# Last two items of a 32-item attention pipeline issued by a hand-written ending, last layer norm done batch by batch

## The chip, the core and the metric

One Trainium2 chip, one of its cores. The engines are PE (TensorE: matmuls and transposes, its weight loads shown as PEld), DVE (VectorE), ACT (ScalarE), POOL (GpSimd) and SP (SyncE, which here only issues DMAs). The metric is the device time of one launch in microseconds (us). A change is called faster or slower when the median moves by over 1%; less than that a measurement of this kernel can hardly tell from none.

## The reference, cut to what is computed

Eight batches of 128 tokens, model width 128, 16 heads. Four attention layers follow each other on `x`; the fourth, `L3`, is where the change lies. Its queries come from `x`, keys and values from `ctx_1024`, and its result goes through a layer norm that is the kernel's output.

```python
qh = jnp.einsum('bsd,hde->bhse', q, Wq) + bq[None, :, None, :]
kh = jnp.einsum('bsd,hde->bhse', k, Wk) + bk[None, :, None, :]
vh = jnp.einsum('bsd,hde->bhse', v, Wv) + bv[None, :, None, :]
scores = jnp.einsum('bhse,bhte->bhst', qh, kh) / scale          # E = 8 numbers a head
attn = jax.nn.softmax(scores, axis=-1)
ctx = jnp.einsum('bhst,bhte->bhse', attn, vh)
out = cat @ Wo + bo
x = q + out
mu = jnp.mean(x, axis=-1, keepdims=True)
var = jnp.mean((x - mu) ** 2, axis=-1, keepdims=True)
return (x - mu) * jax.lax.rsqrt(var + LN_EPS) * gamma + beta
```

## The kernel before

One attention of one batch is an item: `n = 0..31`, layer `n // 8`, batch `b = n % 8`. Items 24 to 31 are L3, and item 31 (`LAST` in the change) is the last. A further layer with 64-number heads runs between items 7 and 8 and is not touched. All engines walk the same list of steps `s`, each with its own in-order instruction stream, and meet by semaphores only; nothing is scheduled at run time. From step 25 on item `n` enters at step `s = n + 1` (step 24 is a hole), and the stages of an item are spread over the steps by the functions `pe_attn`, `act_attn`, `pool_attn` and `dve_attn`:

- step n+1: PE forms the scores in two halves of eight heads, S(n,0) into PSUM banks 0 and 1 and S(n,1) into banks 2 and 3; DVE takes the row maxima of each half (`dve_max`, counted by `max_done`); POOL splits the maxima into three bf16 parts (`pool_split`).
- step n+2: PE turns the split maxima (`pe_mT`, L345), ACT copies them (`act_mrow`), PE forms the transposed scores T(n,0) in banks 4 and 5 (`pe_scores`, L322 the products, L330 the maxima subtracted), ACT takes the exponential (`act_exp`, L415).
- step n+3: T(n,1) goes to the same banks 4 and 5 and so waits until the exponential of T(n,0) has read them; then V(n), the product with the values, 32 matmuls (`pe_V`, L364), into bank 6 for even and 7 for odd items (`o_bank`).
- step n+4: ACT copies the sum out (`act_osum`, L422), PE turns it back (`pe_back`, L372), DVE divides by the row sums (`dve_norm`, L496 and L500), PE turns it once more (`pe_onT`, L377), ACT copies (`act_onT`, L428).
- step n+5: PE multiplies by the output weights (`pe_z`, L381), DVE adds the residual and takes mean and variance (`dve_z` and `dve_stats`, L508, L514, L516).

`free` holds PE back until the maxima of the half that last used a bank are taken, before other work borrows that bank. The queries of L3 are made in pairs of batches at steps 24, 26, 28 and 30 (`pe_proj`, L592, into bank 2): ACT rounds them to bf16 (`act_p0`), DVE forms the rest (`dve_rest`, L666), ACT and DVE the next two parts (L674, L680), and SP and ACT issue the DMAs that stack the parts in `qs` (`stack_dma`, L692). Step 30 makes those of batches 6 and 7, that is of items 30 and 31, so S(30,0) waits for these DMAs.

The final layer norm goes by pairs of batches: at even steps 30 to 36 POOL computes (variance + eps)^-0.5 for two batches (`pool_rstd`, L550 and L552), and at the end of odd steps 31 to 37 DVE's `output(b0)` does two normalisations (L569) and a multiplication and an addition over both batches (L1636, L1638). SP then stores the two batches, 64 KB each (L1055), behind all its other DMAs.

The steps end as they run empty: at step 34 PE has T(31,1), back(30), z(29), onT(30), V(31); at step 35 back(31), z(30), onT(31); at step 36 z(31).

## Time and profile before

| what | value |
|---|---|
| time, median of 3 runs | 343.07 us (342.51 to 345.08) |
| the profiled execution, its own time | 343.29 us |
| its span, first to last instruction | 341.4 us |
| PE / DVE / ACT / POOL busy | 86% / 69% / 62% / 27% |
| granted TensorE clock, mean | 0.982 |

The profile is of one execution. Its span is 1.9 us shorter than that execution's own time, and that time is 0.2 us above the median. Busy shares are averages over layers with different limits; for the change only the last 40 us matter.

### The profile page before, as it was taken

The numbers are of one execution on the slowest core, as the hardware profiler recorded it, in microseconds if no ns is written. First come the engines' busy times: TensorE is split into PE (matmuls) and PEld (weight loads), VectorE is DVE, ScalarE is ACT, GpSimd is POOL, SyncE is SP. The second block draws the span as 40 slices with busy tenths as digits, with TensorE's granted clock in tenths as the row PEclk, the third lists the DMA queues.
The fourth block names the chain that finished last, engine by engine and source line by source line (L and its number), as shares of the span: only waits on it lengthen the run. The fifth ranks groups of instructions, "written<-read, shape, count | busy, mean of one in ns | idle before, by whom it ended". The sixth has DMA issues, their size and how long they took to land.

```text
span 341.4 us, 10348 instructions
## 1 busy us (share of the span) xinstructions
PE 293.8 (86%) x4157; PEld 220.2 (64%) x4157; DVE 236.7 (69%) x480; ACT 212.9 (62%) x463; POOL 92.7 (27%) x261
## 2 busy tenths in 40 slices
PE   7889999988989989988988899889869986996871
PEld 4535657766868768866766676666547764784650
DVE  6566498259886666767766578787886657775855
ACT  4377778666677776876755666457655544555550
POOL 3025353110310000001413734514433304314131
PEclk9999999999999999999999999999998999999896
DMA  6879900000000000001320324312330011011001
GB/s 198 233 182 243 356 6 2 2 2 0 2 2 2 2 0 2 2 0 42 84 64 25 85 80 134 104 49 78 110 93 3 8 44 48 4 46 49 17 18 31
DMA packets 26735, 20.93 MB, mean 61 GB/s; under 512 B 3256, under 2 KB 25664, under 8 KB 26432
## 3 DMA queue, kind: packets, MB, share of 16 engines
q1 hardware_dynamic: 23360, 18.24, 19.0%
q10 hardware_dynamic: 3328, 2.04, 2.1%
q8 instruction: 33, 0.54, 0.7%
q14 instruction: 14, 0.11, 0.1%
HBM read 6.11 MB, written 0.52 MB: 19 GB/s over the span
## 4 chain that ended last, share of the span: by engine, by line
PE 48%; ACT 15%; DVE 12%; issue 7%; POOL 5%; SPq 5%; DMA 4%; ACTq 2%; POOLq 0%
PE psum L364 7%; ACT probs L867 5%; PE psum L825 4%; SPq L692 4%; DMA qs<-part_q 4%; PE psum L791 4%; PE psum L766 4%; PE psum L740 3%; ACT probs L875 3%; PE psum L322 3%; PE psum L337 3%; PE psum L592 3%; PE psum L986 2%; PE psum L802 2%; PE psum L817 2%
## 5 line engine op out<-in xcount | busy, mean ns | idle before, releaser
L489 DVE TENSOR_REDUCE maxs<-psum 128x8 f32<-128x1024 f32 x64 | 77.5, 1213 | 37.4 <-PE psum L337 28.6
L415 ACT ACTIVATE probs<-psum 128x1024 f32<-128x1024 f32 x64 | 65.6, 1025 | 34.6 <-PE psum L330 21.8
L364 PE MATMUL psum<-probs,vpad 128*32 128x128 f32 x1024 | 35.4, 280 | 0.0
L867 ACT ACTIVATE probs<-psum,maxs 128x128 f32<-128x128 f32 x128 | 34.8, 390 | 0.5 <-DVE maxs L916 0.5
L364 PEld LDWEIGHTS psum<-probs,vpad 128*32 128x32 f32 x1024 | 26.6, 111 | 12.0 <-issue 6.9
L337 PE MATMUL psum<-ks,qs 64*128 64x128 bf16 x512 | 25.7, 221 | 9.9 <-DMA qs<-part_q 3.3
L322 PE MATMUL psum<-qs,ks 64*128 64x128 bf16 x512 | 25.7, 221 | 8.4 <-ACT probs L415 8.2
L550 POOL TENSOR_SCALAR rstd<-stats 128x2 f32<-128x2 f32 (+1 forms) x19 | 4.2, 223 | 99.8 <-DVE stats L516 99.7
L322 PEld LDWEIGHTS psum<-qs,ks 64*128 64x128 bf16 x512 | 14.6, 95 | 21.8 <-ACT probs L415 10.8
L926 DVE TENSOR_REDUCE mres<-probs 128x8 f32<-128x1024 f32 x16 | 19.5, 1218 | 12.6 <-ACT probs L867 12.6
L916 DVE TENSOR_REDUCE maxs<-psum 128x8 f32<-128x1024 f32 x16 | 19.5, 1220 | 11.7 <-PE psum L791 11.7
L467 POOL CAST mp<-maxs 128x16 bf16<-128x16 f32 x32 | 6.6, 206 | 74.9 <-DVE maxs L489 74.5
L337 PEld LDWEIGHTS psum<-ks,qs 64*128 64x128 bf16 x512 | 16.8, 96 | 14.8 <-issue 8.1
L330 PE MATMUL psum<-mrow,sel 64*128 64x128 bf16 x512 | 25.2, 219 | 0.0
L875 ACT COPY probs<-psum 128x1024 f32<-128x1024 f32 x16 | 16.7, 1046 | 5.8 <-PE psum L802 5.8
L930 DVE TENSOR_TENSOR probs<-probs,mres 128x1024 f32<-128x1024 f32 x16 | 19.6, 1225 | 0.6
L422 ACT COPY osum<-psum 128x256 f32<-128x256 f32 x32 | 12.1, 377 | 12.5 <-PE psum L364 12.3
L817 PE MATMUL psum<-probs,v1all 128*64 128x128 f32 x256 | 17.5, 279 | 2.3 <-ACT probs L875 1.8
L552 POOL TENSOR_TENSOR rstd<-rstd,small 128x2 f32<-128x2 f32 (+1 forms) x23 | 18.0, 780 | 1.9
L330 PEld LDWEIGHTS psum<-mrow,sel 64*128 64x128 bf16 x512 | 17.8, 95 | 0.5
L766 PE MATMUL psum<-xnT,wmat 128*128 128x256 f32 x64 | 17.4, 400 | 0.3 <-ACT ks L773 0.3
L817 PEld LDWEIGHTS psum<-probs,v1all 128*64 128x64 f32 x256 | 13.7, 136 | 5.9 <-ACT probs L875 4.6
(159 smaller groups left out, 627.8 us busy)
## 6 DMA issues: line engine op xcount, KB each, us to landing
qs<-part_q SPq DMA_DIRECT2D x63, 64.0 KB, 2.0
ks<-part_k SPq DMA_DIRECT2D x30, 128.0 KB, 2.4
ks<-part_k SPq DMA_DIRECT2D x36, 64.0 KB, 2.0
wmat<-in_wmat SPq DMA_DIRECT2D x1, 1856.0 KB, 10.5
qs<-part_q ACTq DMA_DIRECT2D x21, 64.0 KB, 2.2
wmat<-in_wmat SPq DMA_DIRECT2D x1, 1024.0 KB, 7.0
qs<-part_q SPq DMA_DIRECT2D x6, 128.0 KB, 5.2
wrow<-in_wrow SPq DMA_DIRECT2D x1, 704.0 KB, 8.6
```

What stands on the lines that cost most here:

```text
L322: e.matmul(bank(4 + r)[:, bt(c)], ks[M.slot][rows, i, bt(b)], qs[rows, i, bt(b)], start=(c == 0), stop=False, skip_group_check=True)
L330: mm = e.matmul(bank(4 + a)[:, bt(i)], sel[rows, mhalf, i, :], mrow[rows, m % 2, :], start=False, stop=True, skip_group_check=True)
L337: s_mm = e.matmul(bank(2 * half + r)[:, bt(c)], qs[rows, i, bt(b)], ks[L.slot][rows, i, bt(b)], start=(c == 0), stop=L is not L2, skip_gro ...
L364: mm = e.matmul(o_bank(n)[rg(c), bt(half)], vpad[:, n % 2, 4 * half + c, G * a:G * a + G], pt, start=(a == 0), stop=(a == 1), skip_group_c ...
L415: e.activation(probs_of(n, half), bank(4, 2), ACT.Exp, scale=layer(n).scale)\
L489: e.tensor_reduce(maxs[:, n % 2, 8 * half:8 * half + 8], bank(2 * half, 2).rearrange("p (h k) -> p h k", k=P), AX.X, ALU.max, negate=True)\
L766: mm = e.matmul(bank(chunk_bank(i, name, c))[:, t * PAIR:(t + 1) * PAIR], a1[:, 2 * (2 * c + t) + KIND[name], :], src[:, i * PAIR:(i + 1) ...
L817: mm = e.matmul(bank(6)[HD * pp:HD * pp + HD, bt(t)], v1[:, b, h * HD:(h + 1) * HD], pT[:, half, bt(4 * pp + t)], start=True, stop=True)
L867: ins = e.activation(probs[:, half, bt(s)], bank(2 * half, 2)[:, bt(s)], ACT.Exp, bias=maxs[:, b % 2, 8 * half + s:8 * half + s + 1])
L875: e.copy(pT[:, half, :], bank(4, 2)).then_inc(L1("pT_out"), 1)
L916: e.tensor_reduce(maxs[:, b % 2, 8 * half:8 * half + 8], bank(2 * half, 2).rearrange("p (h k) -> p h k", k=P), AX.X, ALU.max, negate=True)\
L930: e.tensor_tensor(p8, p8, rec.unsqueeze(2).broadcast_to([P, 8, P]), ALU.mult).then_inc(L1("norm"), 1)
```

## The change

`LAST = 31`. PE, ACT and DVE leave the common step functions after step 33; three hand-written endings (`pe_end`, `act_end`, the last lines of DVE's stream) issue what is left. T(31,1) is written right behind T(31,0) into banks 0 and 1 in place of 4 and 5, and waits only until the maxima of S(31,0) are taken. V(31) is written into bank 2 in place of 7, its wait for item 29's sum to be read is gone, and its second half alone waits for the second exponential. The two last items then go in pairs: back(30), back(31), onT(30), onT(31), z(30), z(31).

The final norm is regrouped for all of L3's batches. DVE computes (x - mean) * gamma as soon as a batch's statistics are there (`scaled`), POOL computes one batch's factor a step (steps 29 to 36), and DVE's `output(b)` multiplies by it and adds beta; SP stores each batch when it is ready. In steps 29 to 33 `scaled(s - 29)` stands ahead of the query work of `end_of_even` and ahead of the maxima of the second half, and `output(s - 29)` behind them.

```diff
         def probs_of(n, half):
             return probs[:, 2 * (n % 2) + half, :]
 
+        LAST = N_ITEM - 1
+
         def o_bank(n):
-            return bank(6 + n % 2)
+            return bank(2 if n == LAST else 6 + n % 2)
 
         def m_turned(n):
             return bank(3)[:, 0:P // 2].bitcast(BF16)
...
             for what, count in FREED.get((n, half), []):
                 e.wait_ge(what, count)
 
+        def t_bank(n, half):
+
+            return 0 if (n, half) == (LAST, 1) else 4
+
         def T_ready(e, n, half):
+            if (n, half) == (LAST, 1):
+                e.wait_ge(sem("max_done"), 2 * LAST + 1)
+                return
             if n == 0 and half == 0:
                 e.wait_ge(sem("maskbc"), 3)
                 e.wait_ge(*L0.mm_done("q_rest", 2))
...
         def pe_scores(e, n, half, m, mhalf):
 
             if m is not None:
-                M, b = layer(m), m % B
+                M, b, tb = layer(m), m % B, t_bank(m, mhalf)
                 T_ready(e, m, mhalf)
                 for c, r, rows, i in heads(mhalf):
-                    e.matmul(bank(4 + r)[:, bt(c)], ks[M.slot][rows, i, bt(b)], qs[rows, i, bt(b)],
+                    e.matmul(bank(tb + r)[:, bt(c)], ks[M.slot][rows, i, bt(b)], qs[rows, i, bt(b)],
                              start=(c == 0), stop=False, skip_group_check=True)
                 if M is L2:
                     pe_mask(e, 4, 1, False)
...
                 for i in range(4):
                     for a in range(2):
                         rows = slice(HD * a, HD * a + HD)
-                        mm = e.matmul(bank(4 + a)[:, bt(i)], sel[rows, mhalf, i, :], mrow[rows, m % 2, :],
+                        mm = e.matmul(bank(tb + a)[:, bt(i)], sel[rows, mhalf, i, :], mrow[rows, m % 2, :],
                                       start=False, stop=True, skip_group_check=True)
                 mm.then_inc(sem("T_mm"), 1)
             if n is not None:
...
             e.transpose(m_turned(n), mp[:, n % 2, :], identB[:, :]).then_inc(sem("mT_mm"), 1)
 
         def pe_V(e, n):
-            e.wait_ge(sem("exp_done"), 2 * n + 2)
+            if n != LAST:
+                e.wait_ge(sem("exp_done"), 2 * n + 2)
             e.wait_ge(sem("vpad_in"), n + 1)
-            if n >= 2:
+            if n >= 2 and n != LAST:
                 e.wait_ge(sem("z_read"), n - 1)
             if n == 0:
                 e.wait_ge(sem("k_raw"), 3)
...
             if n == B + 1:
                 e.wait_ge(*L2.mm_done("q_rest", 4))
             for half in range(2):
+                if n == LAST:
+                    e.wait_ge(sem("exp_done"), 2 * n + 1 + half)
                 for a in range(2):
                     for c in range(4):
                         pt = probs_of(n, half)[:, bt(2 * c + a)]
...
             for s in steps:
                 n, n1, n2 = at(s, lo, hi), at(s - 1, lo, hi), at(s - 2, lo, hi)
                 n3, n4 = at(s - 3, lo, hi), at(s - 4, lo, hi)
+                if n2 == LAST:
+                    break
                 pe_scores(e, n, 0, n2, 1)
                 ahead(s)
                 if n1 is not None:
...
                 if n4 is not None:
                     pe_z(e, n4)
                 pe_scores(e, n, 1, n1, 0)
+                if n1 == LAST:
+                    pe_scores(e, None, 1, LAST, 1)
                 if n3 is not None:
                     pe_onT(e, n3)
                 odd(s)
...
                     pe_V(e, n2)
 
 
+        def pe_end(e):
+
+            pe_z(e, LAST - 2)
+            pe_V(e, LAST)
+            pe_back(e, LAST - 1)
+            pe_back(e, LAST)
+            pe_onT(e, LAST - 1)
+            pe_onT(e, LAST)
+            pe_z(e, LAST - 1)
+            pe_z(e, LAST)
+
+        def act_end(e):
+
+            act_exp(e, LAST, 1)
+            act_osum(e, LAST - 1)
+            act_osum(e, LAST)
+            act_onT(e, LAST - 1)
+            act_onT(e, LAST)
+
         def act_mrow(e, n):
             e.wait_ge(sem("mT_mm"), n + 1)
             if n >= 2:
...
             e.wait_ge(sem("T_mm"), 2 * n + half + 1)
             if n >= 2:
                 e.wait_ge(sem("V_mm"), n - 1)
-            e.activation(probs_of(n, half), bank(4, 2), ACT.Exp, scale=layer(n).scale)\
+            e.activation(probs_of(n, half), bank(t_bank(n, half), 2), ACT.Exp, scale=layer(n).scale)\
              .then_inc(sem("exp_done"), 1)
 
         def act_osum(e, n):
...
         def act_attn(e, steps, lo, hi, even, odd, first=lambda s, half: None):
             for s in steps:
                 n1, n2, n3 = at(s - 1, lo, hi), at(s - 2, lo, hi), at(s - 3, lo, hi)
+                if n2 == LAST:
+                    break
                 if n3 is not None:
                     act_osum(e, n3)
                 first(s, 0)
...
             for p in range(4):
                 stack_up(e, L3, "q", 2 * p, 2)
             for b in range(B):
-                e.wait_ge(sem("out_ready"), b // 2 + 1)
+                e.wait_ge(sem("out_ready"), b + 1)
                 e.dma_start(out_d[b], xn[:, b, :]).then_inc(sem("stored"), 16)
             e.wait_ge(sem("stored"), 16 * B)
 
...
                     pool_resid(e, "FF", "b_ff", b, 2, "stats_LC", b + 2)
                 if 24 <= s <= 30 and s % 2 == 0:
                     pool_resid(e, "L3", "bo_3", s - 24, 2, "ff_read", (s - 24) // 2 + 1)
-                if 30 <= s <= 36 and s % 2 == 0:
-                    pool_rstd(e, "N3", "L3", "ln", 1e-5, s - 30, 2)
+                if 29 <= s <= 36:
+                    pool_rstd(e, "N3", "L3", "ln", 1e-5, s - 29, 1)
 
             def behind2(s):
                 if s in (9, 11):
...
             pe_proj(e, L2, "k", 4, 2, 7)
             pe_proj(e, L2, "q", 4, 2, 7, PAIR)
             pe_attn(e, range(10, 37), B, N_ITEM, even2, odd2, ahead2)
+            pe_end(e)
 
         @block.scalar
         def _(e):
...
                     act_p1(e, L3, "q", s - 24, 2)
 
             act_attn(e, range(9, 37), B, N_ITEM, even2, odd2, first2)
+            act_end(e)
 
         @block.vector
         def _(e):
...
                 if 23 <= s <= 29 and s % 2:
                     dve_ff(e, (s - 23) // 2)
 
-            def output(b0):
-                bs, n = slice(b0, b0 + 2), b0 // 2
-                dve_xn(e, "N3", "ln", b0, 2)
-                e.wait_ge(sem("xn_N3"), b0 + 2)
-                e.tensor_tensor(xn[:, bs, :], xn[:, bs, :], row("g_3", 2), ALU.mult).then_inc(sem("aff3"), 1)
-                e.wait_ge(sem("aff3"), n + 1)
-                e.tensor_tensor(xn[:, bs, :], xn[:, bs, :], row("b_3", 2), ALU.add).then_inc(sem("out_ready"), 1)
+            def scaled(b):
+                e.wait_ge(sem("stats_L3"), b + 1)
+                e.scalar_tensor_tensor(out=xn[:, b, :], in0=x[:, b, :], scalar=stats[:, b, 0:1],
+                                       in1=row("g_3")[:, 0, :], op0=ALU.subtract, op1=ALU.mult)\
+                 .then_inc(sem("scaled3"), 1)
+
+            def output(b):
+                e.wait_ge(sem("rs_N3"), 2 * b + 2)
+                e.wait_ge(sem("scaled3"), b + 1)
+                e.scalar_tensor_tensor(out=xn[:, b, :], in0=xn[:, b, :], scalar=rstd[:, b:b + 1],
+                                       in1=row("b_3")[:, 0, :], op0=ALU.mult, op1=ALU.add)\
+                 .then_inc(sem("out_ready"), 1)
 
             def odd2(s):
                 if s == 9:
...
                 if 22 <= s <= 28 and s % 2 == 0:
                     for c in (2, 3):
                         dve_relu(e, (s - 22) // 2, c)
-                if 31 <= s <= 37 and s % 2:
-                    output(s - 31)
+                if 29 <= s <= 36:
+                    output(s - 29)
 
             def late(s):
                 if 21 <= s <= 27 and s % 2:
...
                     any_p2(e, LC, "q", s - 15, 2)
 
             def end_of_even(s):
+                if 29 <= s <= 36:
+                    scaled(s - 29)
                 if 24 <= s <= 30 and s % 2 == 0:
                     dve_rest(e, L3, "q", s - 24, 2, 2)
                     any_p2(e, L3, "q", s - 24, 2)
 
-            for s in range(9, 38):
+            for s in range(9, 34):
                 dve_attn(e, [s], B, N_ITEM, even2, odd2, first2, end_of_even)
                 late(s)
+            dve_z(e, LAST - 2)
+            scaled(B - 3)
+            dve_norm(e, LAST - 1)
+            dve_norm(e, LAST)
+            output(B - 3)
+            dve_z(e, LAST - 1)
+            scaled(B - 2)
+            dve_z(e, LAST)
+            scaled(B - 1)
+            output(B - 2)
+            output(B - 1)
 
 
 # ---- launch: one core; the host only lays the arrays out ----
```

## Rows read from the trace of the kernel before

**Rows 1.** The page's chain that ended last, over the whole span, by engine.

```profile
PE 48%; ACT 15%; DVE 12%; issue 7%; POOL 5%; SPq 5%; DMA 4%; ACTq 2%; POOLq 0%
```

**Rows 2.** Windows: busy us of each engine (instructions), granted clock, DMA share, GB/s.

```profile
315.00:320.00 5.00, 3.94 (x62) 3.20 (x66) 3.17 (x7) 2.47 (x4) 0.00 (x0) 0.66 0.01 3
...
316.00:317.00 1.00, 0.94 (x11) 0.75 (x12) 0.29 (x1) 0.13 (x2) 0.00 (x0) 0.50 0.00 0
...
335.00:342.00 7.00, 0.00 (x0) 0.00 (x0) 2.66 (x9) 0.00 (x0) 0.93 (x2) 0.59 0.13 37
```

**Rows 3.** Timeline of the last 15 us: start, duration, what [idle before <-releaser].

```profile
326.40 0.23 PE L345 MATMUL psum<-identB,mp 128*128 128x128 bf16 x1 [0.97 <-POOL mp L472]
...
327.68 1.02 ACT L415 ACTIVATE probs<-psum 128x1024 f32<-128x1024 f32 x1 [0.74 <-PE psum L330]
...
328.84 0.40 PE L322 MATMUL psum<-qs,ks 64*128 64x128 bf16 x8
...
330.80 1.08 PE L364 MATMUL psum<-probs,vpad 128*32 128x128 f32 x32
...
331.94 0.37 ACT L422 COPY osum<-psum 128x256 f32<-128x256 f32 x1 [0.79 <-PE psum L364]
...
334.16 0.49 PE L381 MATMUL psum<-wmat,onT 128*128 128x128 f32 x2 [0.36 <-ACT onT L428]
...
335.14 0.42 DVE L1638 TENSOR_TENSOR xn<-xn,wrow 128x256 f32<-128x256 f32 x1
335.48 0.28 DVE L508 TENSOR_TENSOR x<-psum,resid 128x128 f32<-128x128 f32 x1
...
336.13 0.18 DVE L516 BATCH_NORM_AGGREGATE stats<-stats 128x2 f32<-128x6 f32 x1
336.40 0.22 POOL L550 TENSOR_SCALAR rstd<-stats 128x2 f32<-128x2 f32 x1 [4.08 <-DVE stats L516]
...
337.45 0.60 DVE L569 TENSOR_SCALAR xn<-x,stats,rstd 128x128 f32<-128x128 f32 x2 [1.14 <-POOL rstd L552]
...
338.54 0.42 DVE L1638 TENSOR_TENSOR xn<-xn,wrow 128x256 f32<-128x256 f32 x1
```

**Rows 4.** The line L1055: issue ns min/median/max, first and last start.

```profile
L1055 SPq DMA_DIRECT2D out_x<-xn x8: 332/394/432, 321.9 to 339.4; - x8
```

**Rows 5.** The chain that ended last, 306 to 323 us: start, duration, what.

```profile
306.32 1.20 DVE maxs L489
...
308.83 0.58 PE psum L592 x4
...
311.06 0.47 DVE rest_q L666
...
312.57 3.44 DMA qs<-part_q
316.06 0.63 PE psum L337 x5
...
320.40 0.52 DVE xn L569 x2
...
321.75 0.74 DVE maxs L489
```

**Rows 6.** Timeline, near 46, 88 and 320 us.

```profile
46.61 0.65 DVE L1553 SCALAR_TENSOR_TENSOR xn<-x,stats,wrow 128x128 f32<-128x128 f32 x2
...
46.89 0.22 POOL L469 TENSOR_TENSOR mres<-maxs,mp 128x16 f32<-128x16 f32 x1
...
88.08 1.23 DVE L930 TENSOR_TENSOR probs<-probs,mres 128x1024 f32<-128x1024 f32 x1
88.14 1.74 POOL L552 TENSOR_TENSOR rstd<-rstd,small 128x2 f32<-128x2 f32 x1
...
320.84 0.39 PE L337 MATMUL psum<-ks,qs 64*128 64x128 bf16 x8
```

**Rows 7.** The page's DMA issues: count, KB each, median us to landing.

```profile
qs<-part_q ACTq DMA_DIRECT2D x21, 64.0 KB, 2.2
```

## The prediction, made before the kernel was run

> **What bounds the kernel now.** I read the profile in three steps. First the chain that ended last, by engine: the reader is to see that PE holds about half of it and no other engine a fifth [rows 1], so a PE average says little about the end. Second, windows over the last 40 us. While PE waits for stacked queries near 315 us its granted clock falls to 0.50, its lower level of 1.2 GHz; a mean of 0.66 over 315 to 320 us means some 3.4 us at that level [rows 2]; and in the last 7 us PE does nothing at all while DVE works 2.7 us and POOL 0.9 us [rows 2]. The end is therefore no matter of throughput but one chain of dependent small steps. Third, the timeline from 326 us, to see that chain. The maxima of item 31 reach PE at 326.40. T(31,1) starts at 328.84, right when the exponential of T(31,0) (327.68 to 328.70) has freed the banks; V(31) runs 330.80 to 331.88; z(31) is ready on PE at 334.65, but DVE takes it only at 335.48, because `output(4)` ends just before, at 335.56 with the overlap of the pipeline. Statistics end at 336.31, POOL's factor lets DVE go on at 337.45, `output(6)` ends at 338.96 [rows 3]. The last of the stores is issued at 339.4 [rows 4] and the span ends at 341.4.
>
> **Part 1, the ending on PE and ACT.** T(31,1) moves from 328.84 to right behind T(31,0), which ends near 327.6 (it is done before the exponential that starts at 327.68 [rows 3]). T is two groups of eight products, 0.40 us each as the profile models them [rows 3] and overlapping, so 0.4 to 0.8 us; I take 0.55, as groups of eight issue faster than they drain. It reaches banks 0 and 1, whose maxima were taken by 323 us [rows 5], so this wait is long met. Queued behind it on PE stand onT(29) and V(30), both 0.55 us later; V(30) then ends near 329.5. z(29) follows (0.25 us of PE's time, half of what z(31) shows with its drain [rows 3]), so V(31) starts near 329.75 in place of 330.80. Its first half needs only the exponential of 328.70; its second half comes at 330.3, and the second exponential, which ACT starts after a copy smaller than osum's 0.37, by 329.1, and which takes 1.02 us [rows 3], has ended by then. V(31) ends near 330.85: 1.05 us earlier. From V(31)'s end to z(31) ready took 334.65 - 331.88 = 2.8 us [rows 3]; that chain stays, and item 30's work is woven into its waits, so z(31) is ready near 333.6 (333.5 to 334.1 if each interleaved transpose delays the other).
>
> **Part 2, DVE's order at the end.** `output(4)` no longer stands ahead of z(31). z(30) is ready near 333.1: its turn back starts when V(31) ends at 330.85 and its chain from there is that of item 31 before, from 332.31 (osum's end) to 334.65, 2.3 us [rows 3]. DVE then does z(30) with statistics, 0.83 us (335.48 to 336.31 [rows 3]), and `scaled(6)`, priced by two instructions of the same form that take 0.65 us together, at 0.34 us with its hand-over [rows 6]. So z(31) starts near 334.25, where before it was 335.48: 1.2 us gained, and DVE, not PE, is what is late there. Its statistics end at 335.1. POOL's two instructions plus both hand-overs took 337.45 - 336.31 = 1.14 us [rows 3]; for one batch I take the same, since two numbers a row are already nearly nothing (0 to 0.3 us less is the bound). `scaled(7)`, 0.34 us, lies under POOL's 1.14 and costs nothing; without that cover it would cost its 0.34. `output(7)` starts at 336.25.
>
> Here a row and a rule differ. Where DVE runs the same scalar_tensor_tensor form, POOL's L469 inside it takes 0.22 us, as short as L550 with DVE idle [rows 3, 6]; where DVE runs a long tensor_tensor on two SBUF inputs, POOL's L552 takes 1.74 us, while at the end both of POOL's instructions with their hand-overs take 1.14 [rows 3, 6]. The Trainium skill, page "SBUF — State Buffer", the section on the memory's two separate sides, says that a DVE instruction with two SBUF inputs and a GpSimd instruction that reads SBUF exclude each other for a whole instruction, whoever starts first. By that rule `scaled(7)`, which is released by the same statistics as POOL, would hold POOL up by about 0.3 us on the last chain; by the row of the same form it costs nothing. I go by the row, and hold 0.3 us in the range.
>
> **Part 3, the last norm and its store.** From POOL's factor to the end of `output(6)` took 338.96 - 337.45 = 1.51 us [rows 3]; one `output(7)` takes 0.34 as above: 1.17 us gained. Before, two stores were issued one behind the other after that; batch 6 now goes 0.8 us earlier, and the median issue of 0.39 us is gained [rows 4]. From the last issue to the end of the span stays 341.4 - 339.4 = 2.0 us. Sum of the ending: 1.23 + 1.17 + 0.4 = 2.8 us; that is, the span would end at 338.6. With the bounds above (0.5 for the interleaving on PE, 0.3 for the port, 0.3 of POOL's own time the other way) it is 2.0 to 3.1.
>
> **Part 4, what steps 29 to 33 pay.** The norm's work for batches 0 to 3 was at steps 31 and 33, 1.44 us each: two L569 (0.60), L1636 and L1638 (0.42 each) [rows 3]. Now each step from 29 carries 0.34 + 0.34. Steps 29 and 30, which had none, lie on the chain. At step 29 `scaled(0)` stands ahead of the maxima that start at 306.32; POOL's split, the turn on PE and, behind it on PE's queue, the query product at 308.83 all follow from them [rows 5]. `scaled(0)` must also await the statistics, which the maxima need not (they start 0.1 us before those end), so the price is about 0.38. At step 30 `scaled(1)` stands right ahead of `dve_rest` at 311.06 [rows 5], and the ACT copy, the DMA issues and S(30,0) at 316.06 wait for that: another 0.38. `output(0)` and `output(1)` stand behind the maxima, in time in which DVE idles until PE's next scores, and cost nothing (0.34 each if that idle time is gone). POOL's new factors at steps 29 and 31 stand ahead of the splits, but take about 1.0 us while DVE's maxima take 1.2, so they are hidden; without that cover 1.0 us each.
>
> At step 31 the maxima of S(31,0) start at 321.75, held back by `output(0)` of 320.40 on [rows 5]; S(31,0) itself had ended on PE at 321.23 [rows 6], 0.5 us before. There 1.44 us goes and 0.34 comes, but `scaled(2)` delays the earlier maxima by 0.38 and with them POOL's split: the two nearly cancel, and `scaled(3)` at step 32 adds 0.38 behind a start that is 0.1 to 0.4 earlier. I take +0.15 for these two steps (0 to 0.5). At step 33 `scaled(4)` and `output(4)` fit before item 30 comes back near 331. Last, SP's stores: two now follow directly behind the query DMAs, whose last lands 3.44 us after its issue [rows 5]. No row shows a store beside them; from below it is 0, from above 64 KB, one issue of 0.4 us. I take 0.1.
>
> Sum of the price: 0.38 + 0.38 + 0.15 + 0.1 = 1.0 us (0.5 to 1.7).
>
> **Forecast.** -2.8 + 1.0 = -1.8 us. The profiled execution would go from 343.29 to 341.5; it stood 0.2 above the median, so 341.3 for the median, 0.5% less than before. That is under the 1% that a measurement of this kernel can tell.
>
> **Rivals.**
> (A) The early price is absorbed. The last query DMA took 3.44 us where those from ACT's queue have a median of 2.2 [rows 7]; if something other than DVE's rest sets its landing, the 0.76 us disappears and with the best ending the gain is 2.8 to 3.1: 340.1. For it: that landing is odd. Against: its issue follows ACT and DVE without a gap.
> (B) The ending gives less: the pairwise order on PE makes each item wait for the other's copy and the port rule holds. Then z(31) is 0.5 later and POOL 0.3 later, so 2.0 is gained against 1.0 paid: 342.1. For it: five hand-overs between PE, ACT and DVE in 2.8 us; against: V(31) is a full 1.05 us earlier whatever follows.
> (C) Slower than before. The place is PE's wait for the query DMAs at 314 to 316 us. It grows by 0.8 to 1.2 us, and this wait is what precedes the stretch at clock 0.50. The scores' group takes 0.63 us there, and 0.40 at full clock [rows 3, 5]. If the low level lasts one more stretch of the same 3.4 us, over PE's densest work of step 31 and 32, it costs up to half of it, 1.7 us, and with the price at its upper end of 1.7 the loss of 3.4 exceeds the gain of 2.8: 343.7 (343.07 + 0.6). With that price it decides once the low stretch is over 2.2 us longer. Against: one longer idle stretch has already cost its clock, and the wait's start doesn't move.
> (D) The change doesn't do what it says, T(31,1) or V(31) held by a wait that I overlook: part 1 is gone, part 3 keeps its 1.57 and part 2 perhaps 0.2: 343.07 - 1.8 + 1.0 = 342.3, which looks like B.
>
> **How the numbers follow.** Forecast 0.48, A 0.20, B with D 0.20, C 0.12. The forecast's own band is 340.7 to 341.9. The range takes in A with its lower end and run-to-run scatter of the medians of 0.5 us, and most of B and C: 339.5 to 343.4. Over 1% faster means below 339.64: only the far end of A together with scatter, 0.13. Over 1% slower means above 346.5, which no case reaches alone: 0.03. The rest, 0.84, is within 1%.
>
> **What the changed profile would show.** Right: V(31) starting near 1.05 us after V(30)'s end less z(29), with the second exponential done before its second half; PE's last matmul 1 us or more nearer to the turn of item 31's maxima; one DVE instruction, not four, after the last POOL factor; one store issued at the end; about 12.2 us from that turn to the end of the span, where it was 15.0. Step 29's maxima start 0.4 us later behind their scores, and S(30,0) about 0.8 us later in the span. Wrong: a wait of POOL beside `scaled(7)`, an idle DVE before z(31), or S(30,0) no later than 316.1. The forecast fails if steps 29 to 32 pay over 2 us, or if the clock's low stretch grows.

## The result and the profile after

The change brings the median from 342.9 us (12 runs, 339.25 to 345.08) to 340.83 us (12 runs, 339.59 to 342.52): ratio 0.9949, 95% interval 0.9927 to 0.9971. That is less than the 1% from which a change is called faster here; the interval does leave out 1, so the gain is small but there. The ratio leaves out slow executions and is not the quotient of the medians. A second, later measurement of both kernels gave 0.9927 (0.9886 to 0.9968). The profiled execution took 341.1 us with a span of 339.2; 341.3 was forecast for the median.

First the page's chain that ended last, by engine, and two windows over the stretches of [rows 2] (columns as there).

```profile
PE 45%; ACT 15%; DVE 12%; SPq 7%; issue 7%; DMA 6%; POOL 6%; ACTq 2%; POOLq 0%
```

```profile
315.00:320.00 5.00, 3.06 (x69) 2.37 (x72) 2.32 (x6) 3.37 (x7) 0.85 (x4) 1.00 0.16 44
...
335.00:340.00 5.00, 0.00 (x0) 0.00 (x0) 1.68 (x7) 0.00 (x0) 1.61 (x4) 0.62 0.09 26
```

The low clock of [rows 2] is missing in this execution: 1.00 where 0.66 was, though PE waits as long for its queries (5.00 us from the query rest to S(30,0) in both). From 335 us on PE is idle as before, DVE works 1.68 us there in place of 2.66, and POOL 1.61 in place of 0.93, since it now computes one factor for each batch. Now the timeline of the last stretch, the answer to [rows 3]; lines have moved: L354 is the turn of the maxima (L345 before), L331 T's products, L450 the exponential, L376 V, L457 osum, L393 z, L545 the sum, L553 the statistics, L587 and L589 POOL's factor, L1673 `scaled`, L1680 `output`.

```profile
327.18 0.23 PE L354 MATMUL psum<-identB,mp 128*128 128x128 bf16 x1 [1.21 <-POOL mp L509]
...
328.25 0.39 PE L331 MATMUL psum<-qs,ks 64*128 64x128 bf16 x8
...
328.45 1.03 ACT L450 ACTIVATE probs<-psum 128x1024 f32<-128x1024 f32 x1 [0.74 <-PE psum L339]
...
330.48 1.08 PE L376 MATMUL psum<-probs,vpad 128*32 128x128 f32 x32
...
331.62 0.37 ACT L457 COPY osum<-psum 128x256 f32<-128x256 f32 x1 [0.80 <-PE psum L376]
...
333.33 1.01 PE L393 MATMUL psum<-wmat,onT 128*128 128x128 f32 x4
...
334.69 0.35 DVE L1673 SCALAR_TENSOR_TENSOR xn<-x,stats,wrow 128x128 f32<-128x128 f32 x1
...
334.95 0.28 DVE L545 TENSOR_TENSOR x<-psum,resid 128x128 f32<-128x128 f32 x1
...
335.60 0.18 DVE L553 BATCH_NORM_AGGREGATE stats<-stats 128x2 f32<-128x6 f32 x1
335.82 0.35 DVE L1673 SCALAR_TENSOR_TENSOR xn<-x,stats,wrow 128x128 f32<-128x128 f32 x1
335.87 0.37 POOL L587 TENSOR_SCALAR rstd<-stats 128x1 f32<-128x1 f32 x1
...
336.32 0.56 POOL L589 TENSOR_TENSOR rstd<-rstd,small 128x1 f32<-128x1 f32 x1
336.92 0.35 DVE L1680 SCALAR_TENSOR_TENSOR xn<-xn,rstd,wrow 128x128 f32<-128x128 f32 x1 [0.48 <-POOL rstd L589]
```

T(31,1) begins 0.2 us before the exponential of T(31,0), no longer behind it. Counted from the turn of item 31's maxima, V(31) starts after 3.30 us (4.40 before [rows 3]), DVE takes z(31) after 7.77 (9.08), and the span ends after 12.02 (15.0). One instruction follows POOL's last factor. The line of the stores, answer to [rows 4]:

```profile
L1092 SPq DMA_DIRECT2D out_x<-xn x8: 332/332/1777, 314.1 to 337.3; - x8
```

One store is left at the end: 339.2 - 337.3 = 1.9 us. And the chain from step 29 on, the answer to [rows 5]:

```profile
306.66 0.35 DVE xn L1673
307.02 1.14 DVE maxs L526
...
309.53 0.58 PE psum L629 x4
...
312.14 0.49 DVE rest_q L703
...
313.67 3.42 DMA qs<-part_q
317.14 0.42 PE psum L346 x8
```

`scaled(0)` is itself on the chain. Step 29's first maxima, before and after:

```profile
302.75 1.22 DVE L489 TENSOR_REDUCE maxs<-psum 128x8 f32<-128x1024 f32 x1 [0.91 <-PE psum L337]
...
302.98 1.22 DVE L526 TENSOR_REDUCE maxs<-psum 128x8 f32<-128x1024 f32 x1 [0.91 <-PE psum L346]
```

So 0.23 us is drift from earlier layers; the rest of the shift of rest_q (311.06 to 312.14) is 0.85 us, and S(30,0) passes it on.

Most of what follows is read from five stretches, each the difference of two starts in one profiled execution: **A** from step 29's first maxima to the query rest, **B** from there to S(30,0) (the DMAs), **C** from S(30,0) to the turn of item 31's maxima, **E** from that turn to DVE's sum of item 31, **F** from that sum to the end of the span. A, E and F repeated within 0.1 us wherever the code in them was the same; B did not, and C holds the stretch of low clock where there is one. Each ratio is against the kernel before as measured beside it: on chip 6 for the ending alone, the norm alone, T(31,1) not early and all `scaled` behind, on chip 11 for the rest; for the first row of the change the chip is not known.

| kernel | A | B | C | E | F | E + F | ratio (95%) |
|---|---|---|---|---|---|---|---|
| before | 8.31 | 5.00 | 10.34 | 9.08 | 5.92 | 15.00 | 1 |
| the change | 9.16 | 5.00 | 10.04 | 7.77 | 4.25 | 12.02 | 0.9949 (0.9927 to 0.9971) |
| the change, again | 9.17 | 4.39 | 10.05 | 7.77 | 4.28 | 12.05 | 0.9927 (0.9886 to 0.9968) |
| ending alone | 8.32 | 4.23 | 10.00 | 9.38 | 5.98 | 15.36 | 1.0012 (0.9984 to 1.0040) |
| ending, pairs, DVE's order | 8.31 | 4.30 | 10.00 | 7.38 | 6.06 | 13.44 | 0.9939 (0.9904 to 0.9975) |
| norm alone | 9.17 | 4.20 | 10.05 | 9.32 | 4.29 | 13.61 | 0.9991 (0.9956 to 1.0026) |
| norm alone, DVE's order | 9.16 | 4.82 | 10.48 | 8.48 | 4.26 | 12.74 | 0.9953 (0.9914 to 0.9991) |
| T(31,1) not early | 9.17 | 4.77 | 10.06 | 8.34 | 4.33 | 12.67 | 0.9956 (0.9927 to 0.9985) |
| four more at step 30 | 10.21 | 5.11 | 10.05 | 7.77 | 4.24 | 12.01 | 0.9975 (0.9935 to 1.0014) |
| scaled(0), (1) behind | 8.41 | 5.21 | 10.04 | 7.78 | 4.30 | 12.08 | 0.9893 (0.9862 to 0.9924) |
| all scaled behind | 8.41 | 5.13 | 9.43 | 7.78 | 4.25 | 12.03 | 0.9885 (0.9855 to 0.9916) |
| and the rest first | 7.33 | 3.98 | 9.42 | 7.77 | 4.25 | 12.02 | 0.9830 (0.9785 to 0.9875) |
| and the end's order | 7.32 | 6.14 | 9.43 | 7.38 | 4.31 | 11.69 | 0.9845 (0.9770 to 0.9921) |
| scaled(7) late (one execution) | 9.17 | 4.90 | 11.28 | 7.77 | 4.41 | 12.18 | - |

### The profile page after: what moved, and what is told of

Read it like the earlier page. It is cut to its first block, busy times and chain, and to the rows that moved or that the text cites. A ratio compares the mean times of both kernels' runs of the same rounds, so it can differ in the third digit from the quotient of the medians.

```text
span 339.2 us, 10364 instructions
## 1 busy us (share of the span) xinstructions
PE 291.1 (86%) x4157; PEld 218.2 (64%) x4157; DVE 236.6 (70%) x480; ACT 212.8 (63%) x463; POOL 96.1 (28%) x269
## 4 chain that ended last, share of the span: by engine, by line
PE 45%; ACT 15%; DVE 12%; SPq 7%; issue 7%; DMA 6%; POOL 6%; ACTq 2%; POOLq 0%
SPq L729 6%; PE psum L376 6%; ACT probs L904 5%; DMA qs<-part_q 5%; PE psum L862 4%; PE psum L828 4%; PE psum L803 4%; ACT probs L912 3%; PE psum L629 3%; PE psum L331 3%; PE psum L346 2%; PE psum L1023 2%; PE psum L839 2%; PE psum L854 2%; ACTq L729 2%
## 5 line engine op out<-in xcount | busy, mean ns | idle before, releaser
L450 ACT ACTIVATE probs<-psum 128x1024 f32<-128x1024 f32 x64 | 65.6, 1025 | 33.6 <-PE psum L339 20.7
L587 POOL TENSOR_SCALAR rstd<-stats 128x2 f32<-128x2 f32 (+2 forms) x23 | 6.4, 277 | 104.8 <-DVE stats L553 104.6
L346 PE MATMUL psum<-ks,qs 64*128 64x128 bf16 x512 | 25.0, 216 | 11.5 <-DMA qs<-part_q 4.3
L376 PE MATMUL psum<-probs,vpad 128*32 128x128 f32 x1024 | 34.6, 276 | 0.0
L376 PEld LDWEIGHTS psum<-probs,vpad 128*32 128x32 f32 x1024 | 26.0, 109 | 11.8 <-issue 6.7
L331 PE MATMUL psum<-qs,ks 64*128 64x128 bf16 x512 | 25.4, 219 | 8.6 <-ACT probs L450 8.4
L331 PEld LDWEIGHTS psum<-qs,ks 64*128 64x128 bf16 x512 | 14.5, 94 | 21.5 <-ACT probs L450 11.4
L589 POOL TENSOR_TENSOR rstd<-rstd,small 128x2 f32<-128x2 f32 (+2 forms) x27 | 19.6, 726 | 2.2
L457 ACT COPY osum<-psum 128x256 f32<-128x256 f32 x32 | 12.1, 378 | 11.2 <-PE psum L376 11.1
```

The costliest lines, as they stand in the source:

```text
L331: e.matmul(bank(tb + r)[:, bt(c)], ks[M.slot][rows, i, bt(b)], qs[rows, i, bt(b)], start=(c == 0), stop=False, skip_group_check=True)
L346: s_mm = e.matmul(bank(2 * half + r)[:, bt(c)], qs[rows, i, bt(b)], ks[L.slot][rows, i, bt(b)], start=(c == 0), stop=L is not L2, skip_gro ...
L376: mm = e.matmul(o_bank(n)[rg(c), bt(half)], vpad[:, n % 2, 4 * half + c, G * a:G * a + G], pt, start=(a == 0), stop=(a == 1), skip_group_c ...
L450: e.activation(probs_of(n, half), bank(t_bank(n, half), 2), ACT.Exp, scale=layer(n).scale)\
L589: e.tensor_tensor(rs, rs, small[:, 0:1].broadcast_to([P, nb]), ALU.pow).then_inc(done, 1)
```

## The experiments

The cuts show each kernel against the change; `...` marks lines left out.

**Theory.** The end gains about 3 us from three things (V(31) earlier, DVE's order, one output and store after the last factor), and steps 29 and 30 pay 0.8 us because `scaled` stands there on the chain. **Rivals:** the ending, or the norm, alone holds the gain; the price is absorbed; the price buys a further stretch of low clock.

**The ending alone.** PE's and ACT's hand-written ending with banks 0, 1 and 2; norm, POOL, SP and DVE's order as before.

```diff
-            for s in range(9, 34):
+            for s in range(9, 38):
...
-                if 29 <= s <= 36:
-                    output(s - 29)
+                if 31 <= s <= 37 and s % 2:
+                    output(s - 31)
```

Expected: 

> The hand-written ending of PE and ACT with its two banks, and the final norm by pairs as before. My account: V(31) starts about 1 us earlier, but output(4), 1.5 us of DVE work, still stands between z(30) and z(31), so DVE takes z(31) near where it did and the end gains only what z(30) gains, 0.2 to 0.3 us; nothing is paid at steps 29 and 30. 342.6 to 342.9, ratio 0.999. Rival: the ending is what brought the time, V(31)'s 1.05 us reaches the end by itself: about 341.9, ratio 0.997.

Measured 342.96 us, ratio 1.0012: nothing. V(31) starts 3.30 us after the turn as in the whole change, yet DVE takes z(31) only after 9.38. DVE's timeline of this kernel (L606, L1675 and L1677 are `output(4)`) shows why:

```profile
332.36 0.29 DVE L545 TENSOR_TENSOR x<-psum,resid 128x128 f32<-128x128 f32 x1 [0.64 <-PE psum L393]
...
333.11 0.57 DVE L606 TENSOR_SCALAR xn<-x,stats,rstd 128x128 f32<-128x128 f32 x2
...
334.18 0.42 DVE L1677 TENSOR_TENSOR xn<-xn,wrow 128x256 f32<-128x256 f32 x1
334.52 0.28 DVE L545 TENSOR_TENSOR x<-psum,resid 128x128 f32<-128x128 f32 x1
```

PE has z(31) ready by 333.14; DVE is with `output(4)` until 334.6. A microsecond won on PE is handed to a queue that is not free. E + F even grows, by 0.36 us: z(30) reaches DVE 7.22 us after the turn where it was 6.94, because PE's z(30) now stands behind onT(31), and that waits for item 31's normalisation, which DVE does only after the statistics of item 29.

**The ending with pairs and DVE's order by hand.** As above, but DVE's last instructions in a hand-written order: item 31's normalisation right behind item 30's, and z(31) ahead of `output(4)`.

```diff
             dve_z(e, LAST - 2)
-            scaled(B - 3)
             dve_norm(e, LAST - 1)
             dve_norm(e, LAST)
-            output(B - 3)
             dve_z(e, LAST - 1)
-            scaled(B - 2)
             dve_z(e, LAST)
-            scaled(B - 1)
-            output(B - 2)
-            output(B - 1)
+            output(4)
+            output(6)
...
```

Expected: 

> The ending of PE and ACT with the final norm by pairs, and DVE's last instructions by hand with z(31) ahead of output(4), that is, the ending alone without the DVE work between z(30) and z(31). My account: the ending alone gave nothing because DVE stood there; now z(31) starts about 7.5 us after the turn of item 31's maxima (9.38 in the ending alone), output(4) lies partly under POOL's factor for the last pair, 1.5 us against 1.1, and the rest stays 5.9 + 0.4: 13.8 us from the turn to the end in place of 15.4, ratio 0.996 to 0.997. Rival, PE's order and not DVE's is what holds z(31): 15 us, ratio 1.000.

Measured 341.19 us, ratio 0.9939, E + F 13.44: the order of one engine's last instructions is worth 1.9 us over the ending alone, with the old norm and without any price at steps 29 and 30 (A 8.31). Its ratio cannot be told from that of the whole change. The sums and what follows them:

```profile
332.79 0.29 DVE L545 TENSOR_TENSOR x<-psum,resid 128x128 f32<-128x128 f32 x1 [0.70 <-PE psum L393]
...
333.54 0.27 DVE L545 TENSOR_TENSOR x<-psum,resid 128x128 f32<-128x128 f32 x1
```

With the turn at 326.16, z(30) comes after 6.63 us in place of 7.22: 0.59 from the earlier normalisation of item 31. z(31) follows 0.75 us later in place of 2.16: 1.41 from `output(4)` no longer standing between.

**The norm alone.** The batch-by-batch norm; PE, ACT and the steps of DVE as before.

```diff
-            for s in range(9, 34):
+            for s in range(9, 37):
                 dve_attn(e, [s], B, N_ITEM, even2, odd2, first2, end_of_even)
                 late(s)
-            dve_z(e, LAST - 2)
...
```

Expected: 

> The norm batch by batch on DVE, POOL and SP, with PE's and ACT's steps and banks as before. My account: z(31) is ready on PE as before (334.65 in the time of the profile before) and DVE is free for it, so 0.8 us of the waiting goes, 1.17 of the output pair and 0.4 of the second store: 2.4 us gained, 1.0 paid at steps 29 to 32. 341.5, ratio 0.996. Rival (the ending brought the time): 342.5, ratio 0.999. The ratio of the whole change was 0.9949.

Measured 342.74 us, ratio 0.9991. F is 4.29, so the output and the store gave their 1.6 us; but E is 9.32, where I expected about 8.3. The timeline:

```profile
334.77 0.38 POOL L575 TENSOR_SCALAR rstd<-stats 128x1 f32<-128x1 f32 x1 [1.95 <-DVE stats L541]
335.24 0.57 POOL L577 TENSOR_TENSOR rstd<-rstd,small 128x1 f32<-128x1 f32 x1
335.84 0.35 DVE L1666 SCALAR_TENSOR_TENSOR xn<-xn,rstd,wrow 128x128 f32<-128x128 f32 x1 [0.77 <-POOL rstd L577]
336.11 0.28 DVE L533 TENSOR_TENSOR x<-psum,resid 128x128 f32<-128x128 f32 x1
```

`output(6)` stands ahead of z(31) in the step's order and waits there for POOL; DVE idles 0.77 us with z(31) ready on PE at 335.17. I missed that wait in the expectation.

**The norm alone with DVE's order by hand.** z(31) and `scaled(7)` ahead of `output(6)`; PE and ACT as before.

```diff
...
+            dve_norm(e, LAST - 1)
             dve_z(e, LAST - 2)
             scaled(B - 3)
-            dve_norm(e, LAST - 1)
             dve_norm(e, LAST)
-            output(B - 3)
             dve_z(e, LAST - 1)
             scaled(B - 2)
+            output(B - 3)
             dve_z(e, LAST)
             scaled(B - 1)
```

Expected: 

> The norm alone, PE and ACT in their old steps, but DVE's last instructions written by hand as in the change: z(31) and its statistics ahead of output(6). In the norm alone output(6) stood ahead of z(31) and waited there for POOL's factor, about 1 us. My account: that order holds most of what the ending brings; from the turn of item 31's maxima to the end of the span 12.6 to 12.8 us (13.6 with the norm alone, 12.0 with the whole change), ratio 0.996 to 0.997. Rival, PE's pairing and idle banks are what is needed: 13.3 us or more, ratio 0.998 to 0.999.

Measured E + F 12.74, as expected; ratio 0.9953 (0.9914 to 0.9991), a little under the 0.996 to 0.997 expected but with these inside its interval. The order is worth 0.87 of the 1.59 us between the norm alone and the whole change, PE's ending the other 0.72. The profiled execution took 344.79 us, with the low clock at 320 to 323.5 us, inside C (10.48); E and F lie behind it.

**T(31,1) not early.** Banks 4 and 5 again, T(31,1) at the head of `pe_end`.

```diff
-            return 0 if (n, half) == (LAST, 1) else 4
+            return 4
...
         def pe_end(e):
 
+            pe_scores(e, None, 0, LAST, 1)
             pe_z(e, LAST - 2)
```

Expected: 

> The changed kernel with T(31,1) back in banks 4 and 5 at the head of the hand-written ending, so that it waits for the exponential of T(31,0). My account by the part on PE and ACT (T early is 1.05 us for V(31)) was wrong in its reason if V(31) here starts no more than 0.3 us later: V(30) no longer has T(31,1) ahead of it, and V(31) may start its first half without the second exponential. I expect V(31) to end 0.1 to 0.4 us later and the time 0 to 0.4 us longer, ratio 0.995 to 0.996. Rival, the idle banks are what matters: V(31) ends 1 us later and the ratio is 0.998.

The turn of item 31's maxima and V(31):

```profile
324.93 0.23 PE L351 MATMUL psum<-identB,mp 128*128 128x128 bf16 x1 [1.21 <-POOL mp L505]
...
328.46 1.42 PE L373 MATMUL psum<-probs,vpad 128*32 128x128 f32 x32
```

V(31) starts only 0.23 us later after the turn (3.53) but ends 0.57 later (4.95 against 4.38; 0.1 to 0.4 was expected), since its second half waits for the exponential. E + F grows by 0.65 to 12.67; more than the 0.4 I allowed, less than the rival's 1. The idle banks are thus worth some 0.6 us of V(31)'s 1.1. The rest is left to the order of PE's queue and the split wait of V(31); no run takes these two apart. The times (0.9956 against 0.9949) are too coarse for it.

**Price: scaled(0) and scaled(1) moved behind the maxima, then all five.** The cut is that for all five.

```diff
             def end_of_even(s):
-                if 29 <= s <= 36:
-                    scaled(s - 29)
...
                 if 29 <= s <= 36:
+                    scaled(s - 29)
                     output(s - 29)
```

Expected, for two: 

> The changed kernel with scaled(0) and scaled(1) moved behind the second half's maxima, and scaled(2) to scaled(4) left where they are. My account: the query rest starts 0.75 us earlier after step 29's first maxima (8.4 us in place of 9.16), while from S(30,0) to the turn of item 31's maxima it stays at the 10.0 us of the changed kernel (9.4 with all five moved). Ratio 0.9927. Rival, steps 31 and 32 hold the larger price: ratio 0.9945 or more.

Expected, for all: 

> The changed kernel with scaled(b) of steps 29 to 33 moved from ahead of the second half's maxima to behind them, right ahead of output(b). My account: the two insertions of 0.38 us on the chain to the last query DMAs are gone, S(30,0) comes 0.8 us earlier in the span and the end with it: 340.1 for a before of 343.07, ratio 0.9925 against 0.9949. Rival (price absorbed by the DMA): S(30,0) stays within 0.2 us and the ratio within 0.001 of 0.9949.

With two moved, A falls from 9.16 to 8.41 and C stays 10.04; with all, C falls to 9.43 as well. So the two `scaled` cost 0.75 of the 0.85 us, and moving the later three gains another 0.6 over the change. The 0.10 that is left of A stands at POOL's split of the maxima at step 29, which takes 1.07 us (306.49 to 307.56 with two moved) where it took 0.98 before (307.57 to 308.55). Medians 339.85 and 338.71, ratios 0.9893 and 0.9885; the second is over 1% below the kernel before by both. For two, 0.9927 was expected, 0.75 us less than 0.9949, and lies just outside the interval; counted from the 0.9927 that the change gave on the same chip it would be 0.9905, inside it. For all, A and C give 1.35 us, 0.9910, inside the interval of 0.9855 to 0.9916, where 0.9925 was expected from step 29 and 30 alone.

**Price doubled: four more instructions ahead of the query rest.** Their results are read by nothing.

```diff
+                if s == 30:
+                    for i in range(4):
+                        e.scalar_tensor_tensor(out=rest_k[:, i * P:(i + 1) * P], in0=x[:, 1, :],
+                                               scalar=stats[:, 1, 0:1], in1=row("g_3")[:, 0, :],
+                                               op0=ALU.subtract, op1=ALU.mult)
```

Expected: 

> The changed kernel with four more instructions of scaled's form (written to a buffer that nothing reads any more) right behind scaled(1) at step 30, ahead of dve_rest. They add no output, only DVE time at that place, four times 0.26 us. My account: that place is on the chain, the query rest starts 1.0 us later, S(30,0) 1.0 us later and the time grows by as much: 341.8 for the 340.8 of the changed kernel, ratio 0.998. Rival A (the price is absorbed by the odd landing of the last query DMA): S(30,0) moves by less than 0.3 us, ratio 0.995. Rival C (a longer wait of PE costs another stretch at the lower clock): time grows by 2 us or more, ratio 1.001 and above, with the granted clock of 315 to 325 us near 0.8.

A 10.21, that is 1.05 more; B 5.11 does not absorb it; C unchanged at 10.05; 341.99 us, ratio 0.9975. The dose shows in full; rival A falls. The low clock of this execution lies at 313 to 318 us:

```profile
313.00:318.00 5.00, 3.86 (x65) 2.78 (x65) 1.93 (x4) 2.83 (x5) 1.10 (x5) 0.66 0.25 69
```

It is over by S(30,0) at 317.74, so it costs nothing visible in C. In this one profile the longer wait brought no further stretch; the ratio of 0.9975 over 12 executions also speaks against the rival's 1.001 and above, but its interval ends at 1.0014.

**A better version.** All `scaled` behind, and at step 30 the query rest ahead of item 26's normalisation.

```diff
             def even2(s):
...
+                if s == 30:
+                    dve_rest(e, L3, "q", s - 24, 2, 2)
+                    any_p2(e, L3, "q", s - 24, 2)
...
-                if 24 <= s <= 30 and s % 2 == 0:
+                if 24 <= s <= 28 and s % 2 == 0:
```

Expected: 

> scaled behind the maxima at steps 29 to 33, and at step 30 also the query rest and its third part (L666 and L680 of the kernel before) moved ahead of item 26's normalisation and item 25's sum. My account: the chain to S(30,0) starts on ACT's first part, not on DVE's four small instructions, so the rest starts about 1.1 us earlier, S(30,0) too, and PE's turn of item 26 waits a little but is no later than PE reaches it. Ratio 0.985 to 0.987 against the 0.9885 with scaled alone moved. Rival, the delayed normalisation of item 26 holds PE up by as much: 0.9885 or more.

338.56 us, ratio 0.9830 (0.9785 to 0.9875), from 6 executions: over 1% faster than the kernel before. Against the change the intervals do not meet, but the gain is near 1% (0.9830 against 0.9927 on the same chip). A is 7.33, another 1.08 less. The rest now starts when ACT's first part is there, not DVE's queue; DVE waits for ACT:

```profile
305.53 1.19 DVE L526 TENSOR_REDUCE maxs<-psum 128x8 f32<-128x1024 f32 x1
...
305.70 0.23 POOL L587 TENSOR_SCALAR rstd<-stats 128x1 f32<-128x1 f32 x1 [4.14 <-DVE stats L553]
...
309.28 0.48 DVE L703 SCALAR_TENSOR_TENSOR rest_q<-psum,bcol,part_q 128x256 f32<-128x256 f32 x1 [0.61 <-ACT part_q L680]
```

**The port.** `scaled(7)` behind `output(6)` and behind POOL's first instruction for batch 7; and, on the better version, z(31) also ahead of `scaled(6)`.

```diff
             dve_z(e, LAST)
-            scaled(B - 1)
             output(B - 2)
+            e.wait_ge(sem("rs_N3"), 2 * B - 1)
+            scaled(B - 1)
             output(B - 1)
```

Expected, on the change: 

> The changed kernel with output(6) and then scaled(7) moved behind POOL's first instruction for batch 7, so that no DVE instruction with two inputs in SBUF begins beside it. In the changed kernel that POOL instruction (L587) took 0.37 to 0.39 us wherever scaled started with it, and 0.23 us in the kernel where scaled stood elsewhere. If the shared access is the cause: L587 back to 0.22 us and the stretch from z(31) to the end 4.25 - 0.15 = 4.1 us. Rival, the longer time belongs to the shape of one number a row, or to chance: 0.37 us stays and 4.25 too. One look, read from segments of the profile.

Expected, on the better version: 

> The kernel with scaled and the query rest moved, and besides at the end z(31) ahead of scaled(6), and scaled(7) behind POOL's first instruction for batch 7. z(31) then starts 0.35 us earlier, but POOL's two instructions for batch 6 end only 1.1 us after z(30)'s statistics, so POOL sets the end: from the turn of item 31's maxima to the end 11.75 us in place of 12.02, ratio 0.982 where the kernel without it gave 0.983. Rival, DVE sets the end: 11.5 us.

The first missed its aim: `output(6)` needed no such wait and slid beside L587 in `scaled`'s place, and `scaled(7)` beside L589. Its timeline:

```profile
338.34 0.35 DVE L1680 SCALAR_TENSOR_TENSOR xn<-xn,rstd,wrow 128x128 f32<-128x128 f32 x1
338.41 0.35 POOL L587 TENSOR_SCALAR rstd<-stats 128x1 f32<-128x1 f32 x1
338.80 0.35 DVE L1673 SCALAR_TENSOR_TENSOR xn<-x,stats,wrow 128x128 f32<-128x128 f32 x1
338.85 0.72 POOL L589 TENSOR_TENSOR rstd<-rstd,small 128x1 f32<-128x1 f32 x1
```

L587 stays near its 0.37, with 0.35, and L589 grows from 0.56 to 0.72; F is 4.41 where 4.1 was expected. In the other kernel DVE adds z(31), with one input in PSUM, beside L587, and L587 takes 0.22:

```profile
333.99 0.27 DVE L545 TENSOR_TENSOR x<-psum,resid 128x128 f32<-128x128 f32 x1
334.16 0.22 POOL L587 TENSOR_SCALAR rstd<-stats 128x1 f32<-128x1 f32 x1 [2.22 <-DVE stats L553]
```

Either POOL instruction is thus 0.13 to 0.16 us longer when a DVE instruction with two inputs in SBUF starts 0.05 to 0.07 us ahead of it. The kernel with all `scaled` behind shows both cases in one execution, for batches 2 and 7:

```profile
318.65 1.19 DVE L526 TENSOR_REDUCE maxs<-psum 128x8 f32<-128x1024 f32 x1
318.82 0.22 POOL L587 TENSOR_SCALAR rstd<-stats 128x1 f32<-128x1 f32 x1 [4.25 <-DVE stats L553]
...
333.91 0.35 DVE L1673 SCALAR_TENSOR_TENSOR xn<-x,stats,wrow 128x128 f32<-128x128 f32 x1
333.96 0.37 POOL L587 TENSOR_SCALAR rstd<-stats 128x1 f32<-128x1 f32 x1
```

From 300 us on, in all 14 profiles, POOL's first instruction took 0.37 to 0.39 us each of the 71 times that a `scaled` had started 0.05 or 0.06 us ahead, 0.35 in the one case above, and 0.21 to 0.23 the other 28 times, 16 of them with one number a row. So neither the shape nor chance explains it. In the kernel with both moves E + F was 11.69 (expected 11.75). The median is no better (339.04 against 338.56): B was 6.14 in that profile, and 0.3 us is below what the runs tell.

**The change again.** Expected: 

> The changed kernel once more, beside the others of this call and on their chip. Ratio 0.995 as on the first; if it is below 0.992, the differences between the earlier calls were differences of the chip.

341.2 us, 0.9927, and E + F of 12.05: A, C, E and F agree to 0.03 us (B does not, 4.39 against 5.00) where the ratios differ by 0.002.

## Why the prediction was right

The forecast of 341.3 stands against 340.83, -1.8 against -2.1 us by the medians (-1.75 by the ratio). The stretches of the two profiles give -2.98 for E + F and +0.85 +0.04 for the price, where -2.8 and +1.0 were forecast. By its steps:

- **Part 1, V(31) 1.05 us earlier:** 1.10. That the early T(31,1) is where it comes from holds for about 0.6 of it.
- **Part 2, z(31) taken 1.2 us earlier, DVE being late and not PE:** 9.08 - 7.77 = 1.31. That DVE's order is what holds z(31) is the step the experiments bear out most: without it the ending gave nothing, and the norm 1.4 of 3.0 us.
- **POOL's 1.14 us unchanged:** 336.92 - 335.78 = 1.14, but by luck: two misses of 0.15 us cancel. One number a row makes L589 0.15 us shorter (0.56 for 0.71), and the shared access makes L587 0.15 longer (0.37 for 0.22). That `scaled(7)` costs nothing under POOL's time was wrong, and the wait of POOL beside it, which the prediction named as a sign of being wrong, is there.
- **Row against rule:** I went by [rows 6], POOL's 0.22 us beside the same DVE form. The rows of the changed kernels decide for the other side: 0.37 us for L587 beside `scaled`, 0.22 without it. The Trainium skill's rule ("SBUF — State Buffer", the section "SBUF: two separate sides") agrees with them in kind; the size was half of the 0.3 us that I had worked out from it. The rows also give the size. A held POOL instruction is longer by what the DVE instruction has left to run, less about 0.15 us: 0.30 left and 0.15 to 0.16 longer (L587 beside `scaled`, L589 in the kernel with `scaled(7)` late), 1.17 left and 1.02 longer (L552 in [rows 6], 1.74 for 0.72). That is worked out from these few shapes only. It also fits L469 in [rows 6], which starts when its DVE instruction (46.61, 0.35 us long) has 0.07 us left, and L589 of batch 7 in the change, which starts with 0.11 us of `output(6)` left: neither is longer.
- **Part 3, 1.57 us:** F fell by 5.92 - 4.25 = 1.67.
- **Part 4, 0.38 + 0.38 at steps 29 and 30:** 0.75 by moving them; the whole of A grew by 0.85, the rest being POOL's split, which the prediction left out. Steps 31 to 33, +0.15: C shows 0.04 against the 10.00 of the two kernels with the old norm. Stores beside the query DMAs, +0.1: not told; B was 4.23 to 5.00 in the three kernels without early stores and 3.98 to 6.14 in those with them.
- **Rival A** fell by the doubled dose, **B** and **D** by E + F, which is 12.02 where 12.2 was forecast. Of B the pairwise order did cost something where DVE's order was left as it was (the ending alone). **C** did not come about in the profiles of the change, but its price is real: in the one execution of `scaled(7)` late the mean granted clock was 0.68 and 0.64 over 315 to 325 us, and C was 11.28 in place of 10.04, with the same code in that stretch.

```profile
315.00:320.00 5.00, 3.42 (x61) 2.53 (x52) 2.21 (x3) 2.75 (x5) 1.10 (x5) 0.68 0.26 69
320.00:325.00 5.00, 5.00 (x87) 3.93 (x86) 3.60 (x10) 2.18 (x4) 2.04 (x7) 0.64 0.07 17
```

## What to carry to other kernels

At the end of an in-order pipeline the gain of an earlier producer arrives only if the consumer's queue is free for it: put the last item's work ahead of the output of the items before it, and cost producer and consumer together, since the earlier producer alone showed nothing here (1.0012) and with the consumer's order it gave 0.9939. An engine that idles on average in the earlier steps does not make work pulled forward into them free: ask ahead of which instruction it stands (0.38 us each ahead of the maxima and the query rest, 0.10 for both behind them). When effects are under 1%, compare stretches between named instructions of one profile; the stretches without DMAs and without low clock repeated to 0.1 us, where 12 executions of one kernel spread over some 3 to 6 us and the medians of the kernel before, measured four times, over 0.65.

## What the runs showed of the hardware

The landing of the last query DMAs, same bytes and same issue order on each queue, differed by over 2 us between executions (B 3.98 to 6.14, as much as the whole change is worth). These two extremes are the better version and the one with the end's order, which have the same code up to the ending; each is one profile, and the cause stays open. And the stretch of lower TensorE clock (0.50 granted, 1.2 GHz) falls at different places from one execution to the next: 315 to 319 us before, none there after, 313 to 318 with four more, 316 to 324 in the one execution of `scaled(7)` late. In these PE had just stood idle, but the same idling in the change had no such stretch behind it. It costs 0 to 1.2 us by what it covers. The 10.34 of C before, against 10.00 in the two kernels with the same code in that stretch and full clock, is such a cost; of the span's 2.2 us difference between the two profiles 0.3 is clock.
